# Two attention layers and two expert layers in one program: second attention's norms on ScalarE, value bias on GpSimd, token tables as constants, turns in another order

## What is computed

```python
x = x + tanh(g_xattn[0]) * attention16heads(layernorm(x), ctx, ...)      # L0, 16 heads of 16
x = x + tanh(g_ffn[0])   * ffn8(layernorm(x))                            # L0, 8 experts
x = x + tanh(g_xattn[1]) * attention(layernorm(x), ctx, mask, Wq, Wk, Wv, bq, bk, bv)  # L1, one head
x = x + tanh(g_ffn[1])   * switch(layernorm(x), wg, w1, w2)              # L1, 8 experts

# ffn8: weights of all 8 experts for each token
w  = exp(-dist / 0.1) * in_zone
fb = exp(-dist / 0.3) * top2(fb);  fb = fb / max(sum(fb), 1e-8)
w  = where(sum(w) < 1e-8, fb, w);  w = w / max(sum(w), 1e-8)
out = sum_e w[e] * ((silu(x @ Wg[e]) * (x @ Wu[e])) @ Wd[e])

# attention of L1
softmax(q @ k.T / 16 + mask * -1e9) @ v          # v = ctx @ Wv + bv

# switch: each token goes to one expert, 256 places in each
idx = argmax(x @ wg);  loc = cumsum(onehot(idx)) - 1;  kept if loc < 256
out = gate * (relu(di @ w1[idx]) @ w2[idx])
```

## Time and profile before

| | |
|---|---|
| median of 3 runs | 763.89 us (762.23 to 765.86) |
| the profiled execution | 764.7 us, of which the span of the engines' instructions is 762.9 us |
| TensorE, mean granted clock | 0.921 of full speed |
| busy: PE, DVE, ACT, POOL | 646.4, 521.0, 331.2, 229.1 us |
| chain that ended last | PE 65%, DVE 24%, issue 5%, ACT 2%, DMA 1%, POOL 1% |

### The profile page before, as it was taken

How to read it: one execution, slowest core, us unless ns; L and a number is a source line. 1 busy time by engine, 2 the same in 40 slices (tenths; PEclk the granted TensorE clock), 3 DMA queues, 4 the chain that set the end, 5 groups by cost and what they waited for, 6 DMA issues and landing times.

```text
span 762.9 us, 12648 instructions
## 1 busy us (share of the span) xinstructions
PE 646.4 (85%) x4564; PEld 546.7 (72%) x4564; DVE 521.0 (68%) x1362; ACT 331.2 (43%) x530; POOL 229.1 (30%) x155
## 2 busy tenths in 40 slices
PE   5978598899899899999799889999966931799995
PEld 4656366787678778778688777898855821799995
DVE  6877987677877866866776647479458883466662
ACT  4434155355356456456355325152523321455641
POOL 2444624566532212221014010010031242255542
PEclk9879779899999999999999999999989955799998
DMA  7303303335442242333243424434221141964700
GB/s 225 121 15 127 125 1 139 125 135 211 180 166 83 85 165 84 137 113 125 83 165 113 162 87 152 132 124 146 83 69 43 61 161 43 318 210 153 242 20 26
DMA packets 43463, 94.51 MB, mean 124 GB/s; under 512 B 3519, under 2 KB 24383, under 8 KB 42384
## 3 DMA queue, kind: packets, MB, share of 16 engines
q1 hardware_dynamic: 41344, 87.62, 33.6%
q0 software_dynamic: 2064, 6.16, 2.3%
HBM read 72.94 MB, written 21.04 MB: 123 GB/s over the span
## 4 chain that ended last, share of the span: by engine, by line
PE 65%; DVE 24%; issue 5%; ACT 2%; DMA 1%; POOL 1%; DVEq 0%; SPq 0%; ACTq 0%; POOLq 0%
PE psum L1591 43%; PE psum L2097 6%; PE psum L1668 2%; PE psum L1698 2%; PE psum L1628 2%; PE psum L1662 2%; DVE work L1063 1%; DVE scratch L266 1%; DVE x_all L1079 1%; PE psum L1635 1%; PE psum L1647 1%; DVE work L951 1%; PE psum L1962 1%; PE psum L1893 1%; PE psum L1945 1%
## 5 line engine op out<-in xcount | busy, mean ns | idle before, releaser
L1591 PE MATMUL psum<-arena 128*128 128x256 f32 (+1 forms) x2544 | 446.0, 334 | 33.8 <-DVE x_all L1079 15.6
L1591 PEld LDWEIGHTS psum<-arena 128*128 128x128 f32 x2544 | 384.5, 199 | 78.4 <-DVE x_all L1079 14.8
L2135 POOL TENSOR_TENSOR diag<-neg_ident,work 128x1024 fp32r<-128x1024 f32 x32 | 60.9, 1904 | 249.3 <-DVE work L1010 242.5
L1063 DVE TENSOR_TENSOR work<-work,psum 128x512 f32<-128x512 f32 x64 | 43.9, 686 | 62.1 <-PE psum L1591 57.3
L625 ACT ACTIVATE arena<-work 128x512 fp32r<-128x512 f32 x64 | 40.3, 630 | 90.7 <-DVE work L1063 78.7
L1079 DVE SCALAR_TENSOR_TENSOR x_all<-psum,w_exp,x_all 128x256 f32<-128x256 f32 x128 | 55.9, 479 | 27.7 <-PE psum L1591 26.9
L618 ACT ACTIVATE work<-psum 128x512 f32<-128x512 f32 x64 | 38.2, 597 | 56.8 <-PE psum L1591 56.3
L1068 DVE TENSOR_TENSOR arena<-work,arena 128x512 fp32r<-128x512 f32 x64 | 51.8, 810 | 8.7 <-ACT arena L625 8.2
L2218 POOL TENSOR_TENSOR arena<-work,arena 128x1024 fp32r<-128x1024 f32 x4 | 9.5, 2370 | 151.1 <-ACT arena L641 151.1
L1010 DVE TENSOR_REDUCE work<-psum 128x8 f32<-128x1024 f32 x32 | 39.0, 1220 | 15.7 <-PE psum L1647 15.6
L593 ACT ACTIVATE work<-psum 128x1024 f32<-128x1024 f32 x32 | 32.8, 1026 | 35.4 <-PE psum L1668 32.3
(11 more groups left out here) (194 smaller groups left out, 844.8 us busy)
## 6 DMA issues: line engine op xcount, KB each, us to landing
arena<-kept SPq DMA_DIRECT2D x24, 1024.0 KB, 5.6
work<-in_w SPq DMA_DIRECT2D x16, 1024.0 KB
kept<-arena SPq DMA_DIRECT2D x8, 1536.0 KB, 6.1
arena<-kept SPq DMA_DIRECT2D x24, 512.0 KB, 4.8
work<-in_w SPq DMA_DIRECT2D x8, 768.0 KB, 7.8
slots<-fill POOLq DMA_DIRECT2D x1, 2080.0 KB
work<-in_ctxT SPq DMA_DIRECT2D x8, 256.0 KB, 3.0
work<-in_ctxT SPq DMA_DIRECT2D x4, 512.0 KB, 5.2
```

Source lines behind the costliest of these rows:

```text
L1063: dve.tensor_tensor(gu[i % 2], gu[i % 2], ps[:, UP, :], ALU.mult).then_inc(hm, 1)
L1591: mm = pe.matmul(dst, left(i, k), right(j, k), start=(n == 0), stop=(n == 3 * K2 - 1))
L2135: pool.tensor_tensor(diag, neg_ident[:, :].rearrange("p (o q) -> p o q", o=1).to_broadcast([P, 8, P]), mx[u % 2].rearrange("p (h o) -> p h ...
```

## The change

1. **Routing weights (L0).** `divide_by_sum` is gone. The first normalisation (4 operations) is dropped, and of the second the maximum is dropped and the multiplication merged into the one that writes `w_exp`: 6 DVE operations fewer in each of the 4 groups.
2. **Norms of L1.** `normalise_a` and `normalise_b` (4 operations of 128x256 per group each) move from DVE to ACT; DVE makes a shift column for each. `v1_add` becomes `v1_evict`, a plain copy on ACT; the value bias (times the tanh gate) is added to `x_all` by POOL in `value_bias`, 4 operations of 128x256 per group, and `add_attention` waits for it (`xv`).
3. **Token tables.** `row_numbers`, `tokn` and `own` are gone; the constants hold them for all tiles, and the reciprocal root is written straight to its column of `x_all`. The count of experts comes after `tok_idx`.
4. **Order in turn3.** Transposes and K of the next group's front half go to the end of the turn before; the queries come before the values, the scores before the transposes of norm b; on DVE `mask_and_max` stands before `xb_low`, and `stats_a`/`root_a` at the head.
5. **First expert's weights.** ACT splits both halves inside `turn3(None, 3)`, ahead of `normalise_b(3)`; the low parts are done by DVE (`first_split`), the first half before `pick_expert`, the second after the dispatch has ended; POOL has no split there any more.
6. **Slots** are loaded in three pieces (2, 2 and 12 tiles) and not two (4 and 12).
7. **Expert stage.** `slots_norm` of the next expert stands after the fourth `hidden_low` and not before the first.
8. **Rows out.** The scatter of a unit's first tile waits only for that tile; for the last expert the second tile has a PSUM bank of its own, so that its first tile leaves before PE is done.

```diff
@@ expert_weights (DVE)
-                divide_by_sum(7)
                 seq(dve.tensor_tensor(r[7], r[7], over_e(rs[1]), ALU.mult))
                 seq(dve.tensor_tensor(rt[4], rt[4], rt[7], ALU.add))
-                divide_by_sum(4)
+                seq(dve.tensor_reduce(rs[2], r[4], AX.X, ALU.add))
+                seq(dve.reciprocal(rs[2], rs[2]))
                 if g >= 2:
                     dve.wait_ge(ac, 2 * E * (g - 1))
-                dve.tensor_scalar(w_exp[g % 2], r[4], tgate[:, 2:3], None, ALU.mult).then_inc(s_wexp, 1)
+                dve.scalar_tensor_tensor(w_exp[g % 2], r[4], tgate[:, 2:3], over_e(rs[2]), ALU.mult, ALU.mult
+                                         ).then_inc(s_wexp, 1)
@@ new on ACT
+            def normalise_b(g):
+                act.wait_ge(sb_ok, g + 1)
+                if g:
+                    act.wait_ge(nbt, GB * g)
+                for t in range(g * GB, (g + 1) * GB):
+                    act.activation(xn_b[t % GB], x_all[:, t, 0:D], ACT.Identity, bias=x_all[:, t, D + 1:D + 2],
+                                   scale=x_all[:, t, D:D + 1]).then_inc(nb, 1)
+
+            def v1_evict(g):
+                for c in range(2):
+                    act.wait_ge(pv3, 2 * g + c + 1)
+                    if g:
+                        act.wait_ge(a1, 2 * g)
+                    act.activation(v1[:, 2 * c:2 * c + 2, :], ps[:, 2 + c, :].rearrange("p (b n) -> p b n", b=2), ACT.Copy
+                                   ).then_inc(v1_ok, 1)
@@ turn3 on DVE
             def turn3(ga, gb):
-                attention_gates(gb)
-                if ga is not None:
-                    xa_low(ga)
-                add_attention(gb)
-                moments_b(gb)
-                root_b()
-                normalise_b(gb)
-                if ga is not None:
-                    v1_add(ga)
-                row_numbers(gb)
-                xb_low(gb)
-                if ga is not None:
-                    mask_and_max(ga)
-                if ga is not None and ga + 1 < G:
+                more = ga is not None and ga + 1 < G
+                if more:
                     stats_a(ga + 1, 0)
                     moments_a(ga + 1, 0)
                     root_a(ga + 1, 1)
-                    normalise_a(ga + 1)
+                attention_gates(gb)
+                add_attention(gb)
+                moments_b(gb)
+                root_b(gb)
+                if ga is not None:
+                    mask_and_max(ga)
+                xb_low(gb)
+                if ga is None:
+                    first_split(0, w4_l1.sem)
                 pick_expert(gb)
-                count_experts(gb)
+                slot_and_gate(gb)
                 pick_place(gb)
+                if more:
+                    xa_low(ga + 1)
@@ the expert unit on DVE
-                    if more:
-                        if i == 1:
-                            dve.wait_ge(s_xs[1], 16)
-                        slots_norm(*nxt)
                     for f in range(8):
                         hidden_low(g, i, f)
+                        if more and f == 3:
+                            dve.wait_ge(s_xs[1 + i], 16)
+                            slots_norm(*nxt)
@@ down4 on PE
                 for j in range(2):
+                    bank = 4 if last and j else 4 + i
...
+                    if last and j == 0:
+                        mm.then_inc(d4_first, 1)
```

More of the change, by code:

```diff
@@ L335, in block_kernel @@
         oh1, loc1, dest = sem("onehot_ready"), sem("places_ready"), sem("rows_ready")
-        s_xs = [sem("first_slots_loaded"), sem("other_slots_loaded")]
+        s_xs = [sem(f"{n}_slots_loaded") for n in ("first", "second", "other")]
         s_raw4 = [sem(f"expert1_weights_loaded{i}") for i in range(2)]
@@ L634, in zone_exps, with normalise_a @@
                 act.activation(rt[5], rt[3], ACT.Exp, scale=-1.0 / 0.3).then_inc(r_out, 1)
+            def normalise_a(g):
+                act.wait_ge(sa, g + 1)
+                if g:
+                    act.wait_ge(nat, GB * g)
+                else:
+                    act.wait_ge(x1t, B)
+                for t in range(g * GB, (g + 1) * GB):
+                    act.activation(xn_a[t % GB], x_all[:, t, 0:D], ACT.Identity, bias=shiftA[:, t:t + 1], scale=rstdA[:, t:t + 1]
+                                   ).then_inc(na, 1)
             def ctx3_high(g):
@@ L812, in _ @@
             silu(27, 0)
+            normalise_a(1)
             h_high(27, 0)
@@ L862, in turn3 @@
                 gate_exp(gb)
+                if more:
+                    xa_high(ga + 1)
+                if more:
+                    k1_evict(ga + 1)
+            xa_high(2)
+            k1_evict(2)
             turn3(2, 1)
@@ L1161, in root_a @@
                                 newtonA[:, 0:groups * GB])
[L1163 to L1171 removed]
+                dve.scalar_tensor_tensor(shiftA[:, sel], mvA[:, sel, 0:1].rearrange("p n o -> p (n o)"), -1.0, rstdA[:, sel],
+                                         ALU.mult, ALU.mult).then_inc(sa, groups)
             weights_low(0)
@@ L1380, in xb_low @@
                                       ).then_inc(nb_lo, 1)
-            top, rank, gate, row, place, own = (r3s[i] for i in range(6))
+            top, rank, gate, row, place = (r3s[i] for i in range(5))
             def over8(col):
@@ L1546, in hidden_low, with rows_out @@
                                          ).then_inc(h1_lo.sem, 1)
-            def rows_out(g, i):
-                dve.wait_ge(d4.sem, d4.now(g, i + 1))
+            def rows_out(g, i, last):
+                if last:
+                    dve.wait_ge(d4_first, 1)
+                else:
+                    dve.wait_ge(d4.sem, d4.now(g, i + 1))
                 dve.wait_ge(out_left.sem, out_left.before(g, i + 1))
@@ L1554, in rows_out @@
                 for j in range(2):
+                    if last and j:
+                        dve.wait_ge(d4.sem, d4.now(g, i + 1))
                     row = xs[:, t + j, :] if isinstance(g, int) else xs[:, bass.ds(t + j, 1), :].rearrange("p a c -> p (a c)")
-                    ins = dve.scalar_tensor_tensor(yo[i][j], ps[:, 4 + i, j * D:(j + 1) * D], row[:, D + 2:D + 3],
+                    ins = dve.scalar_tensor_tensor(yo[i][j], ps[:, 4 if last and j else 4 + i, j * D:(j + 1) * D], row[:, D + 2:D + 3],
                                                    row[:, 0:D], ALU.mult, ALU.add)
@@ L1572, in turn @@
                         split_w2(*nxt)
-                    rows_out(g, i)
-            split_w2(0, 0)
+                    rows_out(g, i, last and i == 1)
             dve.wait_ge(s_xs[0], 16)
@@ L2106, in turn @@
                         slots_transposed(*((g, 1) if i == 0 else (g + 1, 0)))
-                    down4(g, i)
+                    down4(g, i, last and i == 1)
             slots_transposed(0, 0)
```

172 lines of the change are left out of this document (84 added, 88 removed).

## The result

The changed kernel took 777.82 us (median of 4 runs, 776.83 to 778.68), the kernel before 763.06 in the same comparison (4 runs, 758.21 to 765.86): a ratio of 1.02 with a 95% interval of 1.0144 to 1.0256. The forecast was 778.0 us, slower than before. The sum came out almost to the point, but several of its terms did not: the expert stage was forecast too short and what stands before it too long, and the two errors nearly cancelled.

A forecast was written before the change was run, and what follows sets the result against it. PE bounds the expert stage, PE and DVE hand work to each other before it, the last turn is a chain. 764.7 - 3.6 - 8.2 - 0.8 - 1.8 = 750.3, + 21.7 (stall) + 6.0 (clock) = 778.0 us; range 763 to 788.

The forecast's parts named there:

- The stall: Expert stage: the late norm is held until POOL's split ends, so PE waits 3.3 us in each of six units.
- The row at 45 us: Old trace: two DVE operations of the norms' form took 2.31 us beside a POOL subtraction; one such takes 0.41.
- The clock: Expert stage: behind each PE stall the clock may fall to half level for 3.4 us, costing 1.7 each.
- I take half, +6.0: Expert stage: clock price set between 0 (no stall lowers it) and 11.9 us (all seven do).
- The rival that had the clock fall in each unit: Expert stage: the clock falls behind every stall, +11.9 us, total 784; chance 0.13.
- The first unit: Expert stage, first expert: norm held to 663.6, the second ends at 664.0, PE done at 662.27: +1.9 us.
- Slots: -0.8: Before the first expert unit: a first piece of 2 tiles instead of 4 saves 0.8 us.
- Routing: Routing weights: chain 1.28 us shorter in each of four groups, -5.1; net -3.6 after giving back 1.5.
- a deduction that the sum does not show: Early groups: POOL's bias additions hold small DVE operations beside them; 1.5 us given back (0 to 4).
- The turns: Last three turns: -2.1, -1.3 and -4.8 from work leaving DVE and a hold removed; sum -8.2 (-3 to -13).
- the hold of 4.2 at the root: Last turn: the DVE operation at 620.63, held by POOL's split, falls from 4.38 to 0.16 us: -4.2.
- The end: Last scatter: first tile leaves while PE works, so one scatter and one operation stay behind PE: about -1.8 us.

The follow-up runs named there:

- e4: Changed kernel with 24 extra 128x256 matmuls on PE ahead of the next expert's transposes, filling the stall: 768.3 us, ratio 1.0071.
- e3b: Changed kernel, late slots_norm kept, with each of POOL's splits waiting for the norm of its own unit: 742.6 us, ratio 0.973.
- e1: Changed kernel with slots_norm back before the first hidden_low: 744.4 us, ratio 0.9754.
- e9: e1 with the slots loaded in two pieces (4 and 12 tiles) and not three: 742.9 us, ratio 0.9718.
- e5: Kernel before with the shorter chain of routing weights alone (6 DVE operations fewer in each group): 755.2 us, ratio 0.988.
- e2: Kernel before with slots_norm alone moved behind the fourth hidden_low: 799.2 us, ratio 1.0481.
- e7: e1 without POOL's value_bias, the value bias left out of the result: 741.3 us, ratio 0.9702.
- e11: e3b with the value bias added by DVE again (v1_add), in place of ACT's copy and POOL's additions: 739.9 us, ratio 0.9697.
- e8: e1 with the low part of the first expert's first weights computed by POOL again, not DVE: 749.5 us, ratio 0.9821.
- e10: e3b with the second expert's weights issued behind the first piece of slots, not the second: 740.9 us, ratio 0.9704.
- e3: Changed kernel, late norm, POOL's split waiting for the norm, but misnumbered so only the first split waited rightly: 772.5 us, ratio 1.0125.

## Why the prediction was right, and where it was not

**The stall: right in place, mechanism and size.** 3.3 for a unit was forecast, 3.00 to 3.21 of idle PE were measured (18.6 in six units), and with the clock held up a unit is 3.3 longer than without the hold (15.66 in e4, 12.33 in e3b). It begins within 0.1 us of where it was put. e1 shows that the norm's move is the cause, e3b that it costs by its overlap with POOL's split and not by its place. The Trainium skill ("SBUF — State Buffer", section "Who interferes with whom") has two sentences that would give opposite outcomes for this operation, by whether it runs in a two-port mode. The one by which the first to issue keeps the shared ports for its whole instruction agrees with each of the seven held norms; the one by which an instruction with at most one SBUF input does not contend says so only outside the two-port modes, and the norm behaved as if it were inside; no run shows the mode itself. The row at 45 us was the better guide, since it had the very form.

**The clock: the wrong step.** "I take half, +6.0" was a mean over two outcomes of old rows. The old trace had a fourth idle time of this kind, 2.83 long, that ended at 374.21, and behind it the level stayed the higher one:

```profile
374.30:377.70 3.40, 2.15 (x17) 1.98 (x18) 2.69 (x5) 0.63 (x1) 1.90 (x1) 1.00 0.17 14
```

So two of four fell, and idle times of one length, 2.83, went both ways. In the changed kernel the fall came in all six full units, at 1.36 each, and not behind the 2.75 of the first unit; e4 puts the clock at 8.5 for the whole stage. The rival that had the clock fall in each unit was right about this, at 1.4 rather than 1.7 for a stall: the granted clock was 0.52 to 0.58 over the 3.4 us behind it, where the old row had 0.50.

**The first unit: half seen.** +1.9 was forecast for the held norm; its unit grew by 3.9. PE's idle times in it are 2.75 for the norm and 1.75 for ACT's wait for weights, and `hidden` itself is 0.8 shorter (6.16 + 1.70 against 8.67). The step "Slots: -0.8" looked at the piece that gets smaller and not at the weights, which the first unit then needs sooner than they come. The gain before the unit was larger (-1.8, of which e9 gives about 1.15 to the pieces), the price was in the unit.

**Routing: right, with a deduction that the sum does not show.** -5.1 was forecast, and the four chains are 5.2 shorter (e5). The table's -1.2 and -5.6 hold more than that, since the profiled execution of the kernel before is 1.8 longer in the second stretch than e2, with the same program there. From the forecast I had subtracted 1.5 for the bias additions on POOL. The changed kernel's stretch is 421.8, e5's 421.9: in the sum they cost nothing there. It may be that other work left DVE in the same stretch; without the additions it is 419.7 (e7) and 418.1 (e11), 0.3 and 1.9 below the shortest kernel with them.

**The turns: right.** -8.2 forecast and -7.7 measured. e8 shows the largest term, the hold of 4.2 at the root: putting POOL's split back returns 2.9. Turn by turn, the distances between the four `tok_idx` went from 38.3, 20.1 and 24.3 to 36.0, 19.6 and 20.2: -2.3, -0.5 and -4.1, where -2.1, -1.3 and -4.8 were forecast. Which edit brought the first two was not tested.

**The end: right**, -1.8 and -1.8.

So the errors were +4.3 in the expert stage (25.9 forecast, 30.2 measured; 2.3 of it in the six units, by the clock, and 2.0 in the first unit) and -3.7 before it (-12.6 and -16.3, start-up included): that 778.0 met 777.8 so closely is partly luck.

The best version of the change is the changed kernel with POOL's split behind the norm, at 740 to 743 us (e3b, e10, e11), 3% under the kernel before; with the norm at its old place (e1) it is 744.4, which the runs do not tell from e3b (739.5 to 745.2).

## What to carry to other kernels

Before moving an operation whose operands all lie in SBUF on DVE, look at what GpSimd runs at the new time: a 0.4 us operation that was issued inside a subtraction of 4.6 us waited for its end here and took up to 4.3 (4.9 in e2). One wait that put the long one behind the short one was enough. Each of the six stalls of about 3 us on TensorE cost 4.7, 3.3 by itself and 1.4 by the clock that fell behind it. And where a load is cut in pieces, follow the next transfer in the queue, and who needs it when, as well as the first piece.

## What was not expected of the hardware

- The last DVE operation that all kernels share ahead of the first routing chain (L951 before) starts at 126.6 us (e3b) to 132.7 (e2), a spread of 6.1 that no edit explains, while undisturbed units of the expert stage repeat to about 0.02 us (12.33 and 12.34). A comparison of spans alone would have given wrong sizes to all the small terms.
- A lead of 0.04 us of POOL over DVE (673.58 and 673.62 in e2) was enough for a hold of the full length.
- In five of the six units of e3 the transposes behind the stall ran at the higher level (0.66 behind 3.06, granted clock 1.00), and the fall came within `down4` (7.48 instead of 6.00, with 0.62 in its first 3.5 us); in the changed kernel it was there from the transposes on (1.11). The unit's length was about the same, 17.1 and 17.0.
